# The verdict on the edge lists moves behind the second block, and the drain takes the last group's order

## The reference

```python
h = relu(layernorm(x))
x = x + gat(h, adj, weight, att)           # wh = h @ weight; softmax over a row's neighbours, 4 heads; att @ wh
h = relu(layernorm(x))
agg = adj @ h
msg = relu(agg @ W_msg.T + b_msg)
gi, gh = msg @ W_ih.T + b_ih, h @ W_hh.T + b_hh
r, z = sigmoid(gi_r + gh_r), sigmoid(gi_z + gh_z)
n = tanh(gi_n + r * gh_n)
x = x + (1 - z) * n + z * h
```

## Time and profile before

| | |
|---|---|
| time, median of 3 runs | 969.53 us (964.33 to 972.71) |
| the profiled execution's own time | 967.29 us |
| its span | 965.5 us |
| mean granted clock of TensorE | 0.838 |
| PE busy | 698.0 us (72%) |
| DVE busy | 747.9 us (77%) |
| ACT busy | 658.5 us (68%) |
| POOL busy | 529.8 us (55%) |
| HBM read | 295.65 MB |

### The profile page before, as it was taken

The page is one execution under the profiler, slowest core; times in us unless marked ns, Lnnn a source line. Parts: engine busy times, 40 slices in busy tenths (PEclk is TensorE's granted clock), DMA queues, the critical chain, the costliest instruction groups (busy, mean ns, idle before and its releaser), DMA issues.

```text
span 965.5 us, 12344 instructions
## 1 busy us (share of the span) xinstructions
PE 698.0 (72%) x3381; PEld 439.4 (46%) x3381; DVE 747.9 (77%) x3128; ACT 658.5 (68%) x667; POOL 529.8 (55%) x518
## 2 busy tenths in 40 slices
PE   1577754768776767667777767786776756899997
PEld 0344432445444434445444444454444554466654
DVE  8485777799887977887878788777887874587774
ACT  1676864879697877878787878687787532455542
POOL 4011117574544637272645576575767775777771
PEclk9897977798887887877778788777877767899998
DMA  9999999799999999999999999999993111233232
GB/s 295 420 420 418 421 424 407 282 410 416 412 416 417 414 418 409 398 410 404 406 394 405 399 405 393 405 378 404 401 403 107 37 34 36 59 86 83 73 81 55
DMA packets 55750, 305.51 MB, mean 316 GB/s; under 512 B 13825, under 2 KB 31442, under 8 KB 39296
## 3 DMA queue, kind: packets, MB, share of 16 engines
q1 hardware_dynamic: 27936, 274.74, 69.9%
q0 software_dynamic: 17152, 23.15, 8.3%
q10 hardware_dynamic: 10592, 6.82, 2.4%
HBM read 295.65 MB, written 12.71 MB: 319 GB/s over the span
## 4 chain that ended last, share of the span: by engine, by line
DMA 44%; PE 23%; ACT 12%; DVE 10%; issue 6%; POOL 4%; ACTq 0%; POOLq 0%; DVEq 0%
DMA adj_in<-in_adj 38%; ACT ind L666 11%; PE ps L927 4%; DMA x<-in_x 3%; PE ps L1143 3%; POOL val L557 2%; PE ps L1166 2%; PE ps L1145 2%; PE ps L1167 2%; PE ps L906 1%; DVE cand L1395 1%; PE ps L1168 1%; PE ps L1161 1%; PE ps L1154 1%; PE ps L1158 1%
## 5 line engine op out<-in xcount | busy, mean ns | idle before, releaser
L666 ACT ACTIVATE ind<-adj_in 128x4096 bf16<-128x4096 int32 x128 | 462.2, 3611 | 80.2 <-DMA adj_in<-in_adj 67.0
L927 PE MATMUL ps<-ind,bit_w 128*128 128x512 bf16 x1024 | 291.7, 429 | 46.7 <-ACT ind L666 46.7
L557 POOL DMA_INDIRECT val<-in_adj,val_idx x144 | 154.4, 1072 | 190.0 <-DVE val_idx L1605 139.5
L539 POOL DMA_INDIRECT rows_in<-wh_table,idx x180 | 193.6, 1076 | 62.2 <-issue 62.2
L927 PEld LDWEIGHTS ps<-ind,bit_w 128*128 128x128 bf16 x1024 | 109.5, 109 | 199.3 <-ACT ind L666 62.5
L617 POOL DMA_INDIRECT adj_in<-g_table,idx x96 | 98.2, 1023 | 34.6 <-issue 29.0
L1395 DVE MAX8 cand<-ps 128x8 f32<-128x256 f32 x256 | 91.0, 417 | 24.3 <-PE ps L927 23.9
L972 PE MATMUL ps<-rows_in,ident 128*128 128x132 f32 x120 | 38.8, 424 | 57.1 <-DVE rows_in L1511 57.1
L580 POOL DMA_DIRECT2D wh_table<-rows_in x16 | 12.2, 760 | 107.8 <-DVE rows_in L1349 107.8
L924 PE MATMUL ps<-idx_r,idx_w 128*128 128x512 bf16 x128 | 60.8, 475 | 11.9 <-ACT ind L666 11.9
L972 PEld LDWEIGHTS ps<-rows_in,ident 128*128 128x128 f32 x120 | 30.5, 310 | 64.4 <-DVE rows_in L1511 64.4
(11 more groups left out here) (299 smaller groups left out, 1520.3 us busy)
## 6 DMA issues: line engine op xcount, KB each, us to landing
adj_in<-in_adj SPq DMA_DIRECT2D x128, 2048.0 KB, 17.8
wh_table<-rows_in POOLq DMA_DIRECT2D x16, 264.0 KB, 8.5
g_table<-t_buf ACTq DMA_DIRECT2D x16, 256.0 KB, 25.6
out<-rows_in SPq DMA_DIRECT2D x16, 256.0 KB, 2.4
rows_in<-wh_table,idx POOLq DMA_INDIRECT x180, 6.6
val<-in_adj,val_idx POOLq DMA_INDIRECT x144, 6.3
adj_in<-g_table,idx POOLq DMA_INDIRECT x112, 2.6
ind<-g_table,idx POOLq DMA_INDIRECT x16, 7.1
```

Source lines behind the costliest of these rows:

```text
L539: nc.gpsimd.indirect_dma_start(out=rows_in[:, s % 2, t, k, :], out_offset=None, in_=wh_table, in_offset=bass.IndirectOffsetOnAxis(ap=idx[: ...
L557: nc.gpsimd.indirect_dma_start(out=val2[:, s, k:k + 1], out_offset=None, in_=adj_values, in_offset=bass.IndirectOffsetOnAxis(ap=val_idx2[: ...
L666: nc.scalar.activation(ind[:, (tile * 2 + half) % IND, :], adj_in[:, slot, 0:b - a].bitcast(I32), ACT.Relu, bias=1.0, scale=-1.0, accum_ou ...
L927: ins = nc.tensor.matmul(o, bit_w[:, b, :], ind[:, (tile * 2 + half) % IND, c0:c0 + HALF], start=False, stop=(b == BITS - 1))
```

## The change

- The verdict goes behind the second block. All engines run the second block without a branch; DVE makes the number (`edges_sound`) after the mix of group 13, PE turns it before the last `rows_back`, and each engine loads it and branches at the end. In place of the verdict, `prepare(q)` waits for the values of its own group.
- The drain has another order on DVE, PE and ACT: group 15's steps stand ahead of the second lists of groups 14 and 15. Some steps get buffers and PSUM banks of their own (`h2_of`, `h2T_of`, `agg_bank`, `ps_tr`, `ps_c`, a third `valid3`) so that groups 13 to 15 don't wait for each other's. The matmuls of `keep_busy` (which only keep PE at work) become shorter (128 columns in place of 512) and fewer. ACT loads tables ahead (`table_for`).
- POOL: the values of group 13 are fetched after the last group's rows (before: ahead of group 14's rows); the last group's first and second neighbours are fetched for three tiles as soon as these are known, then for the fourth tile, then the third rows. The values of groups 14 and 15 are fetched between the high rows of the second block. The low rows of 8 to 15 have their own place (`edges_low`), and the high rows a ring of 11. POOL issues as many gathers in all as before.

```diff
-RING2 = 17
-PRE = 4
+RING2 = 11
...
+        edges_low = arena[:, 0:LOW].rearrange("p (b k d) -> p b k d", b=NG - SCAN_PRE, k=G)
+        edges_in = arena[:, LOW:LOW + RING2 * 5 * D].rearrange("p (b k d) -> p b k d", b=RING2, k=5)
...
             def _(pool):
+                def high_rows(q):
+                    if q >= RING2:
+                        pool.wait_ge(agg2_mm, q - RING2 + 1)
+                    for k in range(SLOTS_OF[0]):
...
                 for s in range(1, NG - 1):
-                    values(s - 1)
+                    if s < NG - 2:
+                        values(s - 1)
                     rows(s)
...
-                pool.wait_ge(ind_done, 2 * T - 3)
-                early_rows(SCAN_PRE)
                 pool.wait_ge(ind_done, 2 * T)
                 pool.wait_ge(idx_done, NG)
-                rows_of_last((0, 1))
+                rows_of_last(range(G - 1), (0, 1))
                 pool.wait_ge(idx_done, NG + 1)
-                rows_of_last((2,))
-                values(NG - 2)
-                early_rows(SCAN_PRE + 1)
-                early_rows(SCAN_PRE + 2)
-                values(NG - 1)
-                early_rows(SCAN_PRE + 3)
-                pool.wait_ge(over_ready, 1)
...
+                rows_of_last((G - 1,), (0, 1))
+                pool.wait_ge(idx_done, NG + 2)
+                rows_of_last(range(G), (2,))
+                values(NG - 3)
+                for q in range(SCAN_PRE, SCAN_PRE + 4):
+                    low_rows(q)
+                for par in range(2):
+                    pool.wait_ge(g_out[par], 16 * (NG // 2))
+                pool.sem_inc(passed_pool, 1)
+                for q in range(NG):
+                    high_rows(q)
+                    if q == 3:
+                        low_rows(NG - 4)
+                    if q == 5:
+                        low_rows(NG - 3)
+                    if q == 6:
+                        values(NG - 2)
+                    if q == 7:
+                        low_rows(NG - 2)
+                    if q == 8:
+                        values(NG - 1)
+                        low_rows(NG - 1)
...
             def _(pe):
-                keep_busy(20)
-                pe.wait_ge(cols2_done, NF)
-                pe.wait_ge(over_done, 1)
-                nc.tensor.transpose(ps[0:1, 3, 0:P], over1[:], ident[:]).then_inc(over_mm, 1)
                 message_columns(NG - 1)
                 message_rows(NG - 1)
...
+                    if q == NG - 2:
+                        pe.wait_ge(cols2_done, NG)
+                        pe.wait_ge(over_done, 1)
+                        nc.tensor.transpose(ps[0:1, 5, 0:P], over1[:], ident[:]).then_inc(over_mm, 1)
                     rows_back(NG - 1)
...
             def _(dve):
                 list_neighbours(NG - 1, (NG - 1) % 2)
+                edge_logits(NG - 3, (NG - 3) % 2)
+                list_edges(NG - 1, (NG - 1) % 2)
                 child_logits(NG - 2, (NG - 2) % 2)
+                edge_indices(NG - 1, (NG - 1) % 2)
+                differences2(NG - 2)
+                row_maximum(NG - 2, (NG - 2) % 2)
                 weigh(NG - 3, (NG - 3) % 2)
...
                     def prepare(q):
                         if q >= 2:
                             dve.wait_ge(agg2_mm, q - 1)
+                        dve.wait_ge(values_in[q % 2], 16 * E2 * (q // 2 + 1))
...
+                    if q + 3 == NG:
+                        edges_sound()
```

More of the change, by code:

```diff
@@ L437, in units, with landed, low_landed, low_rows_of @@
             return (a, a + 1) if m in (4, 8) else (a,) if 1 <= m <= 14 else ()
[L439 to L449, removed]
+        def landed(q):
+            return 16 * SLOTS_OF[0] * (q // RING2 + 1)
+        def low_landed(q):
+            return 16 * SLOTS_OF[1] * (q // SCAN_PRE + 1)
+        def low_rows_of(q):
+            return edges_first[:, q] if q < 4 else edges_more[:, q - 4] if q < SCAN_PRE else edges_low[:, q - SCAN_PRE]
         def rows_of(s):
@@ L491, in _ @@
                 with sp.If(general < 1):
[L492 to L496, removed]
+                    sp.sem_inc(passed_pool, 1)
                 with sp.Else():
@@ L773, in _ @@
                 columns(2)
+                exps(NG - 3)
                 columns(3)
@@ new lines, in _ @@
+                send_lists2(NG - 1)
+                gates_of_h(0)
+                aggregate2(0, (1,))
+                candidate_of_h(4)
+                aggregate2(1, (1,))
+                candidate_of_h(5)
+                pe.wait_ge(hn_done, NF - 1)
+                aggregate2(0, (0,))
+                for q in range(NG):
+                    gates(q)
+                    if q >= 1:
+                        rows_back(q - 1)
+                    if NF <= q + 4 < NG:
+                        turn2(q + 4)
+                    if q + 1 < NG:
+                        aggregate2(q + 1, (1, 0) if q else (0,))
+                        gates_of_h(q + 1)
+                    if q == NG - 2:
+                        pe.wait_ge(cols2_done, NG)
+                        pe.wait_ge(over_done, 1)
+                        nc.tensor.transpose(ps[0:1, 5, 0:P], over1[:], ident[:]).then_inc(over_mm, 1)
@@ L1110, in _ @@
+                rows_back(NG - 1)
                 pe.wait_ge(over_ready, 1)
@@ L1190, in _ @@
-                    pe.wait_ge(hn_done, NF - 1)
-                    aggregate2(0, (0,))
-                    for q in range(NG):
-                        gates(q)
-                        if q >= 1:
-                            rows_back(q - 1)
-                        if NF <= q + 4 < NG:
-                            turn2(q + 4)
-                        if q + 1 < NG:
-                            aggregate2(q + 1, (1, 0) if q else (0,))
-                            gates_of_h(q + 1)
-                    rows_back(NG - 1)
+                    pe.sem_inc(passed_pool, 1)
@@ L1706, in _ @@
[L1706 to L1711 removed]
+                differences2(NG - 1)
+                edges2(NG - 2)
                 def column(a, i):
@@ new lines, in _ @@
+                prepare(0)
+                edges2(NG - 1)
+                restart()
+                for q in (1, 2):
+                    prepare(q)
+                for q in range(NG):
+                    candidate(q)
+                    if q >= 1:
+                        add_rows(q - 1)
+                    mix(q)
+                    if q + 3 < NG:
+                        prepare(q + 3)
+                    if q + 3 == NG:
+                        edges_sound()
+                dve.wait_ge(over_mm, 1)
@@ L1766, in _ @@
[L1766 to L1775 removed]
+                    dve.sem_inc(passed_pool, 1)
                 with dve.Else():
+                    for par in range(2):
+                        dve.wait_ge(out_done[par], 16 * (NG // 2))
```

532 lines of the change are left out of this document (261 added, 271 removed).

## The result

| | before | after |
|---|---|---|
| median of the runs | 967.91 us (4 runs) | 69762.57 us (4 runs, 69748.17 to 69772.24) |
| ratio | | 71.865 (71.5513 to 72.1787) |
| span of the profiled execution | 965.5 us | 69746.0 us |

The account below looks back on a forecast made before the run. PE bounds the second block before; after, POOL's queue starves PE up to group 9, then PE bounds again. 800 + 114.8 + 66.0 + 2 + 1 = 983.8 us span, plus 1.8 around it: 985 us, range 968 to 996.

Parts of the forecast that it names:

- The drain's other chain to S: From group 15's `child_logits` to its messages' landing: under 33 us in place of 39.4, putting the first high row at 802.
- S: Start of the first high row on POOL, 817.97 us before; forecast 800, 18 us earlier.
- the 1 us for the load and the branch: At the end, after the last store, loading `over_i` and branching: 1 us, bounds 0 to 2.
- The rivals: Quicker POOL: 972 us, chance 0.20; gap before gathers closes: 952 us, 0.06; last group's chain not shortened: 997 us, 0.12.
- from S to group 9's high rows: Second block, POOL: 83 gather steps, 111.5 us, plus 3.3 us until PE uses the last: 114.8 us.
- from there to the end, without the branch: PE from group 9's high rows on: 66.0 us without a gap, plus 2 us for its lower clock.
- POOL's queue: In the drain, gathers up to the first high row: through at 798, with some 3 us lost awaiting third rows' indices.
- The starvation at group 9: Second block: PE waits for gathered rows, 16 us at group 9 and 33 us in all.
- The clock: PE has a lower clock after its wait in the second block: 2 us added, bounds 0 to 5.
- The Trainium skill's rule: Two-port VectorE instructions fully block GpSimd: 30 us of POOL held in place of 6, about 1009 us; the forecast rejected it.
- `prepare` that lengthens the gathers: Second block: gathers take up to 1.58 us beside `prepare` in place of 0.94, costing POOL 8.0 us over 14 groups.
- The verdict's 6.7 us: Drain: group 15's messages no longer wait for the verdict, 6.7 us, putting the first high row at 811.3 at latest.

Follow-up runs that it names:

- Experiments 1 to 4: Changed kernel with own masks per group: 991.63 us; without the value test: 993.65; with two steps in old order: 998.11. Kernel before with them exchanged: 69624.58 us.
- experiment 1: The changed kernel with masks `valid2` and `late_place` kept apart for even and odd groups: 991.63 us, ratio 1.0226 to the kernel before.
- experiment 5: On the changed kernel with own masks, the 34 other gathers put later in POOL's queue: 978.95 us, ratio 1.0118 to the kernel before.
- experiments 1, 5 and 7: Changed kernel with own masks: 991.63 us; on that, 34 gathers later in POOL's queue: 978.95; or on it, POOL's and DVE's orders both changed: 968.72.
- Experiment 6: The changed kernel with own masks, without the last branch and the general version: 993.61 us, ratio 1.0227 to the kernel before.
- experiment 9: On the version with own masks and POOL's and DVE's orders changed, the branch ahead of each engine's last step: 961.68 us, ratio 0.9914.
- Experiment 8: The kernel before with the verdict turned behind the last group's messages: 963.97 us, ratio 0.9953.

## Why the prediction was wrong

**The step that failed.** The part "*The drain's other chain to S*" took the new order of DVE as a matter of time alone: the steps overlap, so much less, so much more. I read which buffers were doubled and did not ask which were not. Two steps that were exchanged share two single masks, and the step that reads them was put behind the next group's step that writes them. In the sum this stands as the 1 us for the load and the branch, with 2 as its bound: a verdict of one has no term there, and cost 68.8 ms. The rivals named mechanisms of time, none a verdict of one; and the sentence that the general version "isn't taken with these inputs" I took as a fact of the inputs, when it is one of the lists made from them. Experiments 1 to 4 show it from four sides: with own masks, or without the one test, or with the two steps in the old order, the changed kernel stays out of the general version, and the exchange alone sends the kernel before into it. The number of the missing and the false places is counted, not measured.

**The steps that held.** For the work that I costed, experiment 1 is the kernel to compare with: a span of 989.0 against the sum of 983.8.

| term | forecast | after | experiment 1 |
|---|---|---|---|
| S | 800 | 799.74 | 803.31 |
| from S to group 9's high rows | 114.8 | 113.0 | 112.8 |
| from there to the end, without the branch | 68 | 69.2 | 68.0 |
| load and branch at the end | 1 | (general version) | 4.9 |

(For after, the end without the branch is the last addition's, 979.14, and the 2.8 us of before.)

- S, in the changed kernel, was right to 0.3 us. POOL's queue was through at 797.88 (forecast 798, with 3.30 us of wait for the third rows, forecast 3), and then POOL had 1.86 us to wait, by the program for `g_table`; that chain was forecast at 802. So both chains came out close together, as said. The 0.3 itself is luck: experiment 1, with the same orders, has S 3.6 later, as its stream ended 5.2 later.
- The starvation at group 9 is shown by experiment 5, which takes it away and gains what it should. In the changed kernel its parts were 2.0, 1.4, 10.0, 0.7 and 15.0 us at groups 4, 6, 7, 8 and 9, forecast 4, 10, 3 and 16 at 6 to 9.
- The clock: behind the wait of 15.00 the pair of 512 columns took 1.91 us, the next pair 1.92, the third 1.25, and those behind it 1.02, the two speeds that the earlier trace rows showed; the granted clock was 0.82 in the stretch up to 915 and 0.97 behind it. The 2 us for it are inside the 68 that held.
- A gather took 1.32 us up to group 9 ((112.8 - 3.3) / 83), forecast 1.34. The Trainium skill's rule ("SBUF — State Buffer", "Who interferes with whom") that a two-port instruction of VectorE fully blocks GpSimd would, as an estimate from the eleven groups of `prepare`, have put group 9 at about 939, 24 us later. The trace has 912.74 and does not agree with the full block.
- One reading of the prediction was wrong: it is not `prepare` that lengthens the gathers. The gather of 1.58 us at 840.81 starts as `prepare` ends, and stands beside `candidate`:

```profile
840.38 0.54 DVE L1731 TENSOR_SCALAR adj_in<-iota,edge_row,val 128x512 f32<-128x512 f32 x1
840.83 0.75 DVE L1743 SCALAR_TENSOR_TENSOR list_arena<-ind,bias_in,list_arena 128x512 f32<-128x512 f32 x1
```

  Counted over the 96 gathers of the kernel before: 26 had nothing of DVE but `prepare` beside them and took 0.96 us in the mean, 0.99 at most; 13 had an idle DVE and took 0.94; 30 overlapped the `tensor_tensor` steps of `mix` and took 1.16, up to 1.44. The mean step of 1.325 holds all this, so the sum did not suffer.
- The mis-sized term is the branch: 4.9, 4.5 and 5.7 us in experiments 1, 5 and 7 (their last additions end 7.7, 7.3 and 8.5 ahead of the end, less 2.8), over my bound of 2. I had taken it from POOL's 0.85 us behind an index, a row in which no engine loads a number or branches. Experiment 6 (2.8 us without the branch) and experiment 9 (3.05 with the branch ahead of the last step) show that it is the branch's place.
- The verdict's 6.7 us I put down as "what this part alone gives to S". Experiment 8 gives 3.4, or about 5 with an equal stream, since POOL's queue, 42 gathers from 754 on, is not through earlier.
- The "last 235 us of the span" are 224.5 if the stream ends at 741; nothing in the sum uses them.

So without the shared masks the change is 2.3% slower (1.6 to 3.0), and its span is 5.2 us over the sum: 3.3 more up to S, 2.0 less from there to group 9, and 3.9 more for the load and the branch.

## What to carry to other kernels

When steps of neighbouring groups are exchanged, list every buffer that the moved step reads and find who writes it next in the new order; a buffer that is single was safe only by the old order. A kernel with a slow path should be costed with the question whether its condition can still change, because that is a rival of another size than all waits. And gathers that share one queue are to be put in the order in which their users need them: 34 in the wrong place cost 10 to 13 us here, and a branch at the very end about 5, both without any work being added.

## What was not expected of the hardware

A load of one number and a branch, which took no more than 0.71 us of POOL's time between two gathers in experiment 8, cost 4.5 to 5.7 us where every engine does it as its last act and then jumps over the general version, and 0.3 where the branch stands ahead of a wait of 3.33 us on PE (experiment 9). In the first case SP waits for PE's sequencer for 2.4 to 4.6 us, in the second for 0.2; in experiments 1 and 5 it also waits 3.7 and 3.2 us for its last store, for 1.9 in the kernel before. Whether PE spends it in the load, the branch or in fetching what follows, no run here separates.
